# Six weight splits of each mixture stage placed ahead of the sigmoid and the choice of experts

## The chip, the cores and the metric

The kernel runs on one core of one Trainium2 chip. The metric is the device time of one execution in microseconds (us). An execution is cut by the profiler into the work of the engines: TensorE (PE in the rows, PEld its weight loads), VectorE (DVE), ScalarE (ACT), GpSimd (POOL) and SyncE (SP), which issues most transfers.

## What is computed

x is 4 x 1024 tokens of 256 numbers. Each residual step works on a normalised x:

```
x = x + 0.5 * mixture(layernorm(x))
x = x + attention(layernorm(x))
x = x + 0.5 * mixture(layernorm(x))
x = x + 0.5 * linear(layernorm(x))
x = x + attention_of_16_heads(layernorm(x))
x = x + 0.5 * linear(layernorm(x))

mixture(x):
    scores = sigmoid(x @ w_gate.T)                 # 16 experts, 4 groups of 4
    group  = sum of the two best scores in a group; the 2 best groups are allowed
    w, idx = the 4 best of the allowed scores; w = w / (sum(w) + 1e-6)
    routed = sum over idx of w * (silu(x @ w1.T) * (x @ w3.T)) @ w2.T
    return routed + swiglu of two shared experts
```

The change touches the mixture alone, which runs twice.

## The kernel before, in words

The program is six stages, each ended by a barrier of all engines. Products are made in three passes of a high and a low part of each operand: an operand is rounded into its high part by one engine, and the low part is what is left, subtracted by another. For the weights of a mixture stage this is a **split**: ScalarE copies the staged weights into w_hi (line 532), and GpSimd subtracts w_hi from them into w_lo (line 495). There are 27 loads of 256 KB each (`N_LOADS`), which SyncE issues at line 445 into three staging buffers (`STAGES`), so that load m waits for the low part of load m - 3: `sp.wait_ge(*w_lo(i - STAGES + 2))`.

All engines of a mixture stage follow one list, which `moe_order` writes out; each engine walks through it in order and does its own part of every entry. In it:

- For eight chunks of 512 tokens: norm (DVE, line 185), turn (transposes on PE, line 787; high part by ACT, line 540; low part by DVE, line 705), logit (PE, copied out by ACT at line 546) and back (PE, line 803; copied by DVE, line 709), with three loads and three splits after each of the first seven. Here splits 0 to 20 and loads up to 23 are made.
- sigmoid of all logits (ACT, a table load and one instruction, line 550), which waits for the last copy of line 709.
- route 0, 1 and 2: the choice of groups, of experts and their weights (DVE, lines 584 to 642), prefix: counts by triangular products (PE, lines 811 and 815), place: the slot of each token (DVE, lines 646 to 658). Between them stand unit(0), unit(1), unit(2), which are pieces of the shared experts: up (PE, lines 775 to 777; silu by ACT, line 556, behind a table load of its own; the product by DVE, line 734), turn_h (PE line 862, ACT line 561, DVE line 746) and down (PE; added to x by DVE, line 755).
- loads 24 to 26 and splits 21 to 26. These are the entries that the change moves.
- again and scatter (DVE lines 697 and 185; POOL, indirect transfers at line 505), table (DVE lines 663 to 674), the rest of the shared experts, and then the tiles of routed tokens, whose first fetch waits for the last w_lo and for all scatters.

DVE's route steps are chained: each waits for the one before it (`then`). The first is held by the sigmoid, PE's prefix by `chosen`, and PE's up(0) stands behind the prefix in PE's queue. The wide attention and the other stages don't use `moe_order`.

Of the kernel before, what the change touches and what calls it, by code (L numbers as in the profile page):

```python
# [110 lines left out]
def macaron(nc, x_d, wg_d, w13_d, w2_d, aq_d, ak_d, av_d, fw_d, fb_d, lq_d, lk_d, lv_d, lo_d,  # L111
# [18 lines left out]
    with ctx:  # L130
# [78 lines left out]
        STAGES, XSLOT, GSLOT = 3, 4, 8  # L209
        N_LOADS = NX + NX // 2  # L210
# [32 lines left out]
        def moe_order(fresh, sums):  # L243


            def unit(i):
                out = [("up", i)] if i < NUNIT else []
                if 0 <= i - 1 < NUNIT:
                    out.append(("turn_h", i - 1))
                j = (i - NSH) // 2 + 2  # L250
                if i >= NSH and (i - NSH) % 2 == 0 and j < SORTED:
                    out.append(("turn_x", j))
                if 0 <= i - 2 < NUNIT:
                    out.append(("down", i - 2))
                return out

            nxt = STAGES

            def loads(n):
                nonlocal nxt  # L260
                out = []
                for _ in range(min(n, N_LOADS - nxt)):
                    out += [("load", nxt), ("split", nxt - STAGES)]
                    nxt += 1
                return out

            def turns(n):
                return [("turn", KD * n), ("turn", KD * n + 1)]

            zeros = [("zero", n) for n in range(len(ZERO_TILES))] if fresh else []  # L270
            order = [("load_gate", 0)] + ([("load_x", b) for b in range(1, BATCH)] if fresh else [])
            order += [("load", m) for m in range(STAGES)]
            for c in range(NCH + 2):
                for n in ([0, 1] if c == 0 else [c + 1]):
                    if n < NCH:
                        if fresh and n % CB == 0:
                            order += [("stat", n // CB), ("root", n // CB)]
                        if n == 0:
                            order.append(("split_gate", 0))
                        order.append(("norm", n))  # L280
                if c < NCH:
                    order += turns(c)
                if 1 <= c < NCH + 1:
                    order.append(("logit", c - 1))
                if c >= 2:
                    order.append(("back", c - 2))
                order += zeros[:1]
                zeros = zeros[1:]
                if c < NCH - 1:
                    order += loads(3)  # L290
            order += [("sigmoid", 0), ("route", 0), ("prefix", 0)] + unit(0) + [("route", 1)] + unit(1)
            order += [("route", 2)] + unit(2) + [("place", 0)] + loads(30) + [
                ("split", m) for m in range(N_LOADS - STAGES, N_LOADS)]
            for c in range(4):
                order += [("again", c), ("scatter", c)]
            order += unit(3) + [("table", 0)]
            for c in range(NCH - 2):
                order += turns(NCH + c) + unit(2 * c + 4)
                if c < 4:
                    order += [("again", c + 4), ("scatter", c + 4)]  # L300
                order += unit(2 * c + 5) if c < NCH - 3 else []
            order += [("fetch", j) for j in range(XSLOT)] + [("turn_x", 0), ("turn_x", 1)] + unit(NSH - 1)
            for i in range(NSH, NUNIT + 2):
                order += unit(i)
                j = (i - NSH) // 2 + XSLOT
                if (i - NSH) % 2 and j < SORTED:
                    order.append(("fetch", j))
            if sums:
                for t in range(NT):
                    order += [("gather", t), ("combine", t)]  # L310
            return order

        def moe(fresh, routing, sums):
            order = moe_order(fresh, sums)
            gate_ring = Ring([u for u in order if u[0] in ("logit", "back") or u[0] == "turn" and u[1] < KD * NCH],
                             [psum[:, i, :] for i in range(6)])
# [2091 lines left out]
```

How the kernel before makes its waits and increments, by code:

```python
def macaron(nc, x_d, wg_d, w13_d, w2_d, aq_d, ak_d, av_d, fw_d, fb_d, lq_d, lk_d, lv_d, lo_d,  # L111
# [31 lines left out]
        def then(ins):  # L143
            ins.then_inc(*chain.up())
            dve.wait_ge(*chain.now())
# [1 line left out]
        def end_of_stage(n, kept=()):  # L148
            done = S("stage_done")
            act.activation(sd[0:1, 0:1], ident[0:1, 0:1], ACT.Sqrt)
            for e in (pe, act, dve, pool, sp):
                e.drain().then_inc(*done.up())
            for e in (pe, act, dve, pool, sp):
                e.wait_ge(*done.now())
            S.next_stage(kept)
# [13 lines left out]
        def act_root(at, n):  # L170
            act.wait_ge(*S("variance")(n))
            act.activation(sd[:, at], ve[:, at], ACT.Sqrt).then_inc(*S("root").up())
# [1 line left out]
        def dve_rsqrt(at, n, out):  # L174
            dve.wait_ge(*S("root")(n))
            then(dve.reciprocal(recip[:, at], sd[:, at]))
            then(dve.tensor_tensor(newton[:, at], recip[:, at], recip[:, at], ALU.mult))
            then(dve.tensor_tensor(newton[:, at], newton[:, at], ve[:, at], ALU.mult))
            then(dve.tensor_scalar(newton[:, at], newton[:, at], -0.5, 1.5, ALU.mult, ALU.add))
            then(dve.tensor_tensor(out[:, at], recip[:, at], newton[:, at], ALU.mult))
# [13 lines left out]
        pool.memset(ident[:, :], 0.0).then_inc(*S("const").up())
        pool.wait_ge(*S("const")(1))
        pool.affine_select(out=ident[:, :], in_=ident[:, :], compare_op=ALU.not_equal, fill=1.0, base=0,
# [1217 lines left out]
                def on_dve():  # L1415
# [48 lines left out]
                            dve.wait_ge(*ulp_ok(c + first))
```

## Time and profile before

| | us |
|---|---|
| median of 3 runs | 2512.88 |
| lowest and highest | 2509.45, 2513.04 |
| the profiled execution's own time | 2509.05 |
| its span, first to last instruction | 2507.3 |
| busy PE, DVE, ACT, POOL | 2107.8, 1532.2, 954.3, 308.9 |
| mean granted TensorE clock, as a share of full | 0.905 |

The span is shorter than the execution's time by 1.75 us of start and end. Busy times are sums over stages with different limits: the stretch in question is two times some 55 us, in which PE idles much. Times in rows are counted from the span's start; the first mixture stage's choice of experts lies at 61 to 105 us, the second's at 946 to 989 us.

### The profile page before, as it was taken

What the parts mean: (1) busy time and instruction counts of PE and PEld (TensorE: products, weight loads), DVE (VectorE), ACT (ScalarE), POOL (GpSimd) and SP (SyncE); (2) the same over time, 40 slices, a digit from 0 to 9 for tenths busy, and PEclk for the clock granted to TensorE, in tenths of its full rate; (3) what the DMA queues carried; (4) which work ended last, traced back from release to release, by engine and by line L of the source; (5) the groups of instructions that cost most, each with busy time, mean ns of one, the idle gap of its engine ahead of it and who ended that gap; (6) DMA issues with size and microseconds to landing.
All of it is one profiled execution on the core that took longest, in us unless ns stands there. A gap on an engine that the chain in (4) does not pass through costs nothing.

```text
span 2507.3 us, 37607 instructions
## 1 busy us (share of the span) xinstructions
PE 2107.8 (84%) x13066; PEld 1605.4 (64%) x13066; DVE 1532.2 (61%) x3628; ACT 954.3 (38%) x1765; POOL 308.9 (12%) x280
## 2 busy tenths in 40 slices
PE   5589999966999974899999736759999899899757
PEld 3478888855888953788888624625555455555445
DVE  7744334346555577444334399677788687688386
ACT  4122233222333342233223234306656556556532
POOL 4320000022000033300000151211101101100000
PEclk8799999988999996999999856679999999999956
DMA  8120111111000031201111130162242332422001
GB/s 265 41 67 25 30 27 31 29 51 42 1 1 1 1 98 50 78 20 31 29 29 31 44 94 9 38 89 52 53 52 53 62 42 53 70 34 28 4 24 51
DMA packets 84026, 114.77 MB, mean 46 GB/s; under 512 B 12212, under 2 KB 73816, under 8 KB 80728
## 3 DMA queue, kind: packets, MB, share of 16 engines
q1 hardware_dynamic: 77416, 94.80, 17.3%
q0 software_dynamic: 6432, 17.57, 2.2%
q8 instruction: 115, 1.88, 0.3%
q14 instruction: 63, 0.52, 0.1%
HBM read 69.16 MB, written 43.17 MB: 45 GB/s over the span
## 4 chain that ended last, share of the span: by engine, by line
PE 67%; DVE 20%; ACT 5%; DMA 3%; issue 3%; POOL 2%; SPq 0%; ACTq 0%; POOLq 0%; DVEq 0%
PE psum L775 10%; PE psum L777 10%; PE psum L776 10%; PE psum L126 5%; PE psum L2316 5%; PE psum L2295 4%; PE psum L127 4%; PE psum L128 4%; PE psum L2267 4%; PE psum L862 3%; DVE m L2178 2%; DVE stats L160 2%; PE psum L2299 2%; DVE xn L185 2%; PE psum L2271 2%
## 5 line engine op out<-in xcount | busy, mean ns | idle before, releaser
L740 DVE SCALAR_TENSOR_TENSOR h<-psum,xg,sg 128x128 f32<-128x128 f32 x592 | 166.8, 345 | 415.3 <-PE psum L862 415.3
L2142 ACT ACTIVATE pt<-psum 128x512 f32<-128x512 f32 x576 | 315.5, 597 | 241.1 <-DVE psum L2220 147.3
L2178 DVE TENSOR_REDUCE m<-psum 128x1 f32<-128x512 f32 (+2 forms) x576 | 377.8, 683 | 39.8 <-PE psum L2267 33.4
L556 ACT ACTIVATE sg<-psum 128x512 f32<-128x512 f32 x180 | 107.7, 598 | 574.6 <-PE psum L777 574.6
L775 PE MATMUL psum<-w_hi,xt_hi 128*128 (+1 forms) x720 | 285.8, 397 | 32.8 <-DVE xt_lo L705 32.8
L776 PE MATMUL psum<-w_lo,xt_hi 128*128 (+1 forms) x720 | 283.9, 394 | 0.0
L777 PE MATMUL psum<-w_hi,xt_lo 128*128 (+1 forms) x720 | 283.8, 394 | 0.0
L2267 PE MATMUL psum<-ks,qs 96*128 96x512 bf16 (+3 forms) x768 | 242.7, 338 | 24.4 <-DMA ks<-qk_scr 12.4
L2295 PE MATMUL psum<-qs,ks 99*128 99x512 bf16 (+3 forms) x768 | 234.8, 331 | 11.4 <-ACT pt L2142 6.6
L775 PE MATMUL psum<-w_hi,ht_hi 128*128 (+1 forms) x720 | 218.1, 303 | 0.3
L777 PE MATMUL psum<-w_hi,ht_lo 128*128 (+1 forms) x720 | 204.0, 283 | 0.0
L776 PE MATMUL psum<-w_lo,ht_hi 128*128 (+1 forms) x720 | 202.7, 282 | 0.0
L775 PEld LDWEIGHTS psum<-w_hi,xt_hi 128*128 128x128 f32 x720 | 136.9, 190 | 58.9 <-issue 35.7
L2295 PEld LDWEIGHTS psum<-qs,ks 99*128 99x128 bf16 x768 | 69.3, 98 | 154.2 <-ACT pt L2142 95.3
L777 PEld LDWEIGHTS psum<-w_hi,xt_lo 128*128 128x128 f32 x720 | 136.6, 190 | 29.9
L776 PEld LDWEIGHTS psum<-w_lo,xt_hi 128*128 128x128 f32 x720 | 137.1, 190 | 22.8
L2316 PE MATMUL psum<-pt,v 128*17 128x512 f32 (+3 forms) x1536 | 151.5, 490 | 0.0
L776 PEld LDWEIGHTS psum<-w_lo,ht_hi 128*128 128x128 f32 x720 | 137.3, 191 | 0.0
L775 PEld LDWEIGHTS psum<-w_hi,ht_hi 128*128 128x128 f32 x720 | 136.7, 190 | 0.6 <-issue 0.6
L777 PEld LDWEIGHTS psum<-w_hi,ht_lo 128*128 128x128 f32 x720 | 136.5, 190 | 0.0
L2271 PE MATMUL psum<-band_q,ident_q 128*128 128x256 bf16 (+1 forms) x512 | 136.0, 272 | 0.0
L2299 PE MATMUL psum<-band,ident_r 128*128 128x256 f32 (+1 forms) x576 | 135.7, 337 | 0.0
(285 smaller groups left out, 4298.8 us busy)
## 6 DMA issues: line engine op xcount, KB each, us to landing
xg<-w_dram SPq DMA_DIRECT2D x54, 256.0 KB, 3.2
qk_scr<-parts SPq DMA_DIRECT2D x32, 384.0 KB, 2.5
qs<-qk_scr SPq DMA_DIRECT2D x96, 128.0 KB, 7.1
ks<-qk_scr SPq DMA_DIRECT2D x96, 128.0 KB, 7.7
xg<-rows_in SPq DMA_DIRECT2D x74, 132.0 KB, 2.2
rows_out<-yb SPq DMA_DIRECT2D x74, 128.0 KB, 1.7
x<-x_dram SPq DMA_DIRECT2D x4, 1024.0 KB, 8.9
out_dram<-x SPq DMA_DIRECT2D x4, 1024.0 KB, 4.5
```

Source lines behind the costliest of these rows:

```text
L126: pe.matmul(out, ai(ah), bi(bh), start=first, stop=False)
L740: ins = dve.scalar_tensor_tensor(out=h[i % 2][:, e, :], in0=u[:, e, :], scalar=xg[j % XSLOT][:, at:at + 1], in1=sg[i % 2][:, e, :], op0=AL ...
L775: pe.matmul(out, a[0], b[0], start=first, stop=False)
L776: pe.matmul(out, a[0], b[1], start=False, stop=False)
L777: return pe.matmul(out, a[1], b[0], start=False, stop=last)
L2142: act.activation(pt[n % NPT][:, :], st_bank(n), ACT.Exp).then_inc(*exped.up())
L2178: dve.tensor_reduce(m3[:, h, at:at + (n - 1) * step + 1:step], mx_ring.bank((kind, i)).rearrange("p (n k) -> p n k", k=wide), AXIS.X, ALU. ...
L2267: ins = pe.matmul(bank[:, o:o + c1 - c0], qs[r][0:KS_ROWS, h, t * P:(t + 1) * P], ks[r][0:KS_ROWS, h, c0:c1], start=True, stop=not near)
L2271: ins = pe.matmul(bank[:, o + w - bw - c0:o + w - c0], tables.ident_q[:, :], band_q[:, u % NHG * HG + h, 2 * P - bw:2 * P], start=False, s ...
L2295: ins = pe.matmul(bank[:, o:o + wide], ks[r][:, h, j * P:(j + 1) * P], qs[r][:, h, q0:q0 + wide], start=True, stop=not by_pe)
L2299: ins = pe.matmul(bank[:, o:o + near], tables.ident_r[:, :], band[:, part, u % NHG, h, b0:b0 + near], start=False, stop=(part == 1))
L2316: ins = pe.matmul(y_banks[c][h * MQ:h * MQ + DH + 1, BANK - wide:BANK], v1[b % 2][:, j, g * HG + h, :], slot[:, o:o + wide], start=(j == F ...
```

## The change

Loads 24 to 26 and splits 21 to 26 come directly after the eight chunks, ahead of the sigmoid, in both mixture stages (the same code makes both). Nothing is added or taken away.

```diff
                 if c < NCH - 1:
                     order += loads(3)
+            order += loads(30) + [("split", m) for m in range(N_LOADS - STAGES, N_LOADS)]
             order += [("sigmoid", 0), ("route", 0), ("prefix", 0)] + unit(0) + [("route", 1)] + unit(1)
-            order += [("route", 2)] + unit(2) + [("place", 0)] + loads(30) + [
-                ("split", m) for m in range(N_LOADS - STAGES, N_LOADS)]
+            order += [("route", 2)] + unit(2) + [("place", 0)]
             for c in range(4):
```

`loads(30)` gives what is left, three loads with splits 21 to 23; the list behind it adds splits 24 to 26.

The queues of PE, DVE, POOL and SP hold the same instructions in the same order as before, since none of these engines has other work between the two places that the splits or loads would pass. Only ACT's queue differs. The first difference, in the first mixture stage at the end of the chunks (line 550 is the sigmoid, and w_in0 to w_in2 are the semaphores of the three staging buffers' loads):

```order
 L540 ACTIVATE xt_hi<-psum 128x512 [waits turned,logit] x2
 L546 ACTIVATE logit_t<-psum 16x512 [waits logit,backed] x2
+L532 ACTIVATE w_hi<-xg 128x512 [waits w_in0]
+L532 ACTIVATE w_hi<-xg 128x512 [waits w_in1]
+L532 ACTIVATE w_hi<-xg 128x512 [waits w_in2]
+L532 ACTIVATE w_hi<-xg 128x512 [waits w_in0]
+L532 ACTIVATE w_hi<-xg 128x512 [waits w_in1]
+L532 ACTIVATE w_hi<-xg 128x512 [waits w_in2]
 L550 ACT_TABLE_LOAD
 L550 ACTIVATE xn<-logits 128x512 [waits logit_ok]
```

The six copies now stand between the last copy of logits and the sigmoid with its table load. The second difference, in the same stage where they stood (sg is the silu of up(2) and up(3), ht_hi the high part of turn_h(1) and turn_h(2)):

```order
 L556 ACTIVATE sg_30<-psum 128x512 [waits up,su]
 L561 ACTIVATE ht_hi<-psum 128x512 [waits h_turned]
-L532 ACTIVATE w_hi<-xg 128x512 [waits w_in0]
-L532 ACTIVATE w_hi<-xg 128x512 [waits w_in1]
-L532 ACTIVATE w_hi<-xg 128x512 [waits w_in2]
-L532 ACTIVATE w_hi<-xg 128x512 [waits w_in0]
-L532 ACTIVATE w_hi<-xg 128x512 [waits w_in1]
-L532 ACTIVATE w_hi<-xg 128x512 [waits w_in2]
 L556 ACTIVATE sg_31<-psum 128x512 [waits up,su]
 L561 ACTIVATE ht_hi<-psum 128x512 [waits h_turned,down]
```

The silu of up(3) now follows turn_h(1) directly. The second mixture stage shows the same two differences.

## Rows read from the trace of the kernel before

**Rows 1.** Stretches: window, us, busy PE PEld DVE ACT POOL, PEclk, DMA share, GB/s
```profile
100.00:116.00 16.00, 5.65 (x24) 4.95 (x24) 15.45 (x50) 1.79 (x3) 6.91 (x7) 0.50 0.14 51
```

**Rows 2.** Chain of work, first stage's sigmoid: start us, us, what
```profile
61.16 0.59 ACT logit_t L546
...
61.76 1.28 ACT L550
...
63.06 0.64 ACT xn L550
...
63.79 0.42 DVE xn L584
```

**Rows 3.** Timeline of SyncE, loads 21 to 23: start us, us, what
```profile
57.27 2.79 SPq L445 DMA_DIRECT2D xg<-w_dram  x3
```

**Rows 4.** Timeline of ACT, first stage, splits 21 to 26
```profile
86.44 1.66 ACT L532 ACTIVATE w_hi<-xg 128x512 fp32r<-128x512 f32 x3
91.23 0.63 ACT L532 ACTIVATE w_hi<-xg 128x512 fp32r<-128x512 f32 x1 [3.13 <-DMA xg<-w_dram]
...
93.94 0.63 ACT L532 ACTIVATE w_hi<-xg 128x512 fp32r<-128x512 f32 x1 [0.59 <-DMA xg<-w_dram]
94.48 0.58 ACT L556 ACTIVATE sg<-psum 128x512 f32<-128x512 f32 x1
```

**Rows 5.** Timeline of ACT, second stage, the same splits
```profile
970.94 1.66 ACT L532 ACTIVATE w_hi<-xg 128x512 fp32r<-128x512 f32 x3
...
978.58 0.63 ACT L532 ACTIVATE w_hi<-xg 128x512 fp32r<-128x512 f32 x1 [0.80 <-DMA xg<-w_dram]
```

**Rows 6.** Timeline of POOL, first stage, low parts of splits 21 to 26
```profile
87.14 3.77 POOL L495 TENSOR_TENSOR w_lo<-xg,w_hi 128x512 fp32r<-128x512 f32 x3 [27.43 <-ACT w_hi L532]
91.94 1.26 POOL L495 TENSOR_TENSOR w_lo<-xg,w_hi 128x512 fp32r<-128x512 f32 x1 [1.02 <-ACT w_hi L532]
93.44 2.66 POOL L495 TENSOR_TENSOR w_lo<-xg,w_hi 128x512 fp32r<-128x512 f32 x2 [0.23 <-ACT w_hi L532]
```

**Rows 7.** Chain of work, first stage, route 2 on DVE
```profile
89.84 1.12 DVE logit_t L626
...
92.10 1.65 DVE xn L630
...
93.83 1.12 DVE xn L632
...
94.97 1.22 DVE xn L634
...
96.21 0.23 DVE xn L634
...
98.93 0.70 DVE xn L640
```

**Rows 8.** Timeline of DVE, second stage, the same steps
```profile
974.35 1.10 DVE L626 TENSOR_SCALAR logit_t<-logit_t 128x32 f32<-128x32 f32 x1
...
976.60 1.64 DVE L630 TENSOR_TENSOR xn<-xn,logit_t 128x512 f32<-128x512 f32 x1
...
978.31 1.10 DVE L632 COPY xn<-xn 128x32 f32<-128x32 f32 x1
...
979.45 1.46 DVE L634 TENSOR_TENSOR xn<-xn 128x32 f32<-128x32 f32 x2
```

**Rows 9.** Chain of work, first stage: prefix, and where matmuls grow short
```profile
70.58 0.33 PE psum L811
...
75.92 0.43 PE psum L777
...
76.86 0.23 PE psum L777
```

**Rows 10.** Closing linear stage: chain by line, 2375 to 2508 us; busy time
```profile
by line: PE psum L126 16.6%; PE psum L1539 11.9%; PE psum L128 9.8%; PE psum L127 9.7%; DVE amax L1445 7.3%; DVE centred L1468 5.2%; DVE xt_lo L1491 4.2%; issue 3.8%; DVE x L1496 3.6%; ACT centred L1396 3.6%; DVE inv L1453 2.2%; DVE centred
...
2400.00:2425.00 25.00, 17.56 (x63) 13.80 (x61) 21.45 (x30) 9.06 (x17) 0.00 (x0) 0.57 0.00 1
```

## The prediction

> **What bounds the kernel now.** I read the stretches first, to see who fills the time after the chunks. Between 100 and 116 us DVE is busy for 15.45 of 16 us while PE works 5.65 [rows 1]: the choice of experts is a chain of DVE steps, and PE, ACT and POOL wait for it. So what counts here is when that chain starts and how fast it runs.
>
> The chain of work shows where it starts. ACT loads the sigmoid's table at 61.76, the sigmoid runs at 63.06, DVE's first step follows at 63.79 [rows 2]. The table load begins the moment ACT is through with the last logits; nothing lies between it and the sigmoid but its own 1.28 us. Anything that is put ahead of it in ACT's queue moves the whole chain, and with it the prefix on PE at 70.58 [rows 9] and up(0), which stands behind the prefix.
>
> Then the timelines of ACT and POOL, for what is moved. In the old place the six copies begin at 86.44 and the last begins at 93.94 for 0.63 us [rows 4], in the second stage 970.94 and 978.58 [rows 5]. Three copies find their data there (1.66 us together); the other three wait, since a staging buffer is loaded again only after its low part is made: POOL takes 3.77 us for three of them [rows 6] and a load needs some 3 us, so that ACT idles 3.13 us ahead of the fourth [rows 4]. Nobody waits for ACT meanwhile: the silu at 94.48 is of up(3), whose product DVE takes up only after route 2 and place.
>
> Last, DVE's steps beside POOL's three pieces of work, 87.14 to 90.9, 91.94 to 93.2 and 93.44 to 96.1 [rows 6]. A subtraction of 128x32 takes 1.12 us, a product of 128x512 1.65, a copy of 128x32 1.12 and a sum of 128x32 1.22, while the next sum of the same form takes 0.23 and a product of 128x512 at 98.93 0.70 [rows 7]. Each of the long ones ends just as a POOL piece ends. The second stage has the same four [rows 8]. DVE is held up by POOL's subtractions here, on the path.
>
> **The change, part by part.**
>
> *The sigmoid's delay.* The six copies now run at 61.76, where the table load ran. Loads 21 to 23 were issued from 57.27 within 2.79 us [rows 3], so the third was out at about 59.7, and with 3 us from issue to copy it is there at 62.7, when ACT comes to it (61.76 + 2 x 0.55). Splits 21 to 23 find their data, as before. Splits 24 to 26 wait for POOL and the loads as before, because nothing in that trip depends on the place. So ACT is held for as long as before: 93.94 + 0.63 - 86.44 = 8.13 us in the first stage, 978.58 + 0.63 - 970.94 = 8.27 in the second. Before, the table load began with no gap, so the sigmoid is late by all of it: **16.4 us** in both stages. No work covers it: DVE has nothing between its last logits and the sigmoid, PE's next entry is the prefix, and POOL's next after the splits is the scatter, which needs place. Bounds: if each of the three waiting loads came 0.3 us later than in the old place, 17.0 in all would be the upper end (an estimate from the 2.8 to 3.1 us that the trips take in rows 4 and 6); if the trip had no cost at all, six copies of 0.55 would be left, 3.3 a stage, 6.6 in all. I take 16.4, since it is the same sequence of instructions with the same waits.
>
> *The relief of DVE.* POOL's three pieces move with the copies. They begin 0.7 us after the first copy and end 9.66 us after it (96.10 - 86.44), so at 71.4, while the late sigmoid ends at about 71.8; DVE waits for the sigmoid all that time and loses nothing. In the old place it gets back, first stage: 1.12 - 0.23, 1.65 - 0.70, 1.12 - 0.23 and 1.22 - 0.23, which is 3.72 us [rows 7]; second stage: 1.10 - 0.23, 1.64 - 0.70, 1.10 - 0.23 and 1.46 - 0.46 for the two sums together, 3.68 [rows 8]. Together **7.4 us**. For the subtraction and the copy the short price is that of the nearest step of that size, the 0.23 of the sum. Bounds: 0, if POOL was not the cause, and 8.3 if the short steps took nothing but 0.1. I take 7.4.
>
> *What is late next.* Before, DVE ran without a gap from route 2 to the low parts ahead of the shared experts' next unit; it still does, 8.13 - 3.72 = 4.4 us later. Scatters start from the same chain. The experts' fetches and the last w_lo aren't nearer to the path: w_lo is early by more than before.
>
> *SP and POOL.* Loads 24 to 26 are issued some 25 us earlier, past no other transfer. Nothing.
>
> *PE's clock.* PE idles through all of DVE's first steps, 63.79 to 70.58 [rows 2, 9]; then its matmuls come at 0.43 us until about 76.3, at 0.23 from there [rows 9]: PE starts at the lower of its two levels (1.2 and 2.4 GHz) and rises 5.8 us later. The pause grows by 8 us, and the start is at the lower level again. When exactly it rises may differ: a us earlier or later is worth half a us on the path, and there are four such starts (two a stage), so about 2 us either way. I take 0.
>
> The sum: 16.4 - 7.4 = 9.0 us longer. The profiled execution took 2509.05, 3.8 us under the median; against its own time this gives 2518.1. From the median of 2512.88 it is **2521.9 us**, and I forecast that.
>
> A rule that would make it worse. ACT's table load takes 1.28 us and begins at once behind the last copy, 61.16 + 0.59 [rows 2]. The Trainium skill, ScalarE: Activation LUTs, section What ACT_TABLE_LOAD costs, adds some 1.38 us of drain to a switch of tables. The row shows none, and by that rule the sum would be some 2.8 us larger if the drain were hidden before and isn't now.
>
> **The rivals.**
>
> 1. *DVE's stalls have another cause* (the steps are slow by themselves). Then only the 16.4 us count: 2529.3. Against it: the long steps end with POOL's pieces, and the same forms take 0.23 and 0.70 when POOL rests [rows 6, 7]. 4%.
>
> 2. *A pause in ACT ahead of a table load*, which a long queue of copies brings out: 1.4 us a stage, 2524.7. The rows have no gap, there too behind a copy [rows 2]. 4%.
>
> 3. *No change, because the trip gets cheap.* If loads 24 to 26 were in place when ACT comes to them, 6.6 - 7.4 leaves 0.8 us of gain, 2512.1. POOL's 1.26 us and the load's 3 us stand against it, and SyncE can't issue earlier than the low part is made. 3%.
>
> 4. *No change, because of the clock.* If PE came out of all four pauses at the higher level, it would save at most half of 5.8 us each time, 11.6 us: 2510.3. Longer pauses speak against it. 3%.
>
> 5. *Faster, by the clock of the closing linear stage.* There PE has 48.0% of the chain over 133 us, 64 us, and at 2400 to 2425 us the granted clock is 0.57 though PE is busy 17.56 of 25 us [rows 10]. Matmuls at 0.23 in place of 0.43 [rows 9] would take 30 us off: 2491.9. It decides from where a good half of these matmuls ran at the higher level, since the kernel is faster than before once more than 9.0 us come off, and by over 0.2% from 14. What speaks for it is only that the stage begins 9 us later and that clock and work might fall together otherwise; against it, its pauses come from its own waits and move along. 3%.
>
> That the change doesn't do what it says is ruled out by ACT's queue, which shows it.
>
> **How the numbers follow.** A measurement of this kernel can tell about 0.2%, 5.0 us, from no change: below 2507.9 is faster, up to 2517.9 the same. The forecast has 83%. Of that I put 7 into the band of no change: the three runs lie between 2509.45 and 2513.04, and from the lowest, with 2 us of luck in the clock, it ends at 2516.5. So faster 3% (rival 5), the same 3 + 3 + 7 = 13%, slower 76 + 4 + 4 = 84%. The range goes from 2515.5 (lowest run, 9.0 more, the clock's 2 and 1 us of the relief's upper end less) to 2527 (highest run, 9.0, the clock's 2, rival 2's 2.8); rival 1 and the cases of no change lie outside.
>
> **What would show it.** In the profile after: six copies at line 532 from about 61.8 with idle ahead of the fourth of some 3.1 us; the table load at about 69.9; the prefix at 78.7; lines 626, 630, 632 and 634 at 0.2 to 0.7 us each; the end of the first choice of experts 4.4 us later; and the span some 9 us longer, with all that follows the second choice moved alike. I am wrong if the copies take under 5 us, if the four steps stay at 1.1 to 1.7, or if the second attention or a linear stage changes its length by over 3 us.

## The result and the profile after

The changed kernel takes 2515.74 us (median of 12 runs, 2511.93 to 2520.59). The kernel before, run beside it, takes 2507.95 (12 runs, 2499.69 to 2513.04; the three runs of the table above are among the twelve, and among the slower of them). The ratio is 1.0032, with a 95% interval of 1.0021 to 1.0043: 8.0 us slower (5.3 to 10.8). The profiled execution took 2520.59 us with a span of 2518.8, 11.5 more than the span before.

ACT's timeline of the changed kernel, first stage, from the last copy of logits on (start us, us, then the instruction), which answers to [rows 2, 4]:

```profile
63.59 0.59 ACT L546 ACTIVATE logit_t<-psum 16x512 f32<-16x512 f32 x1 [3.34 <-PE psum L777]
64.09 1.65 ACT L532 ACTIVATE w_hi<-xg 128x512 fp32r<-128x512 f32 x3
68.88 0.63 ACT L532 ACTIVATE w_hi<-xg 128x512 fp32r<-128x512 f32 x1 [3.14 <-DMA xg<-w_dram]
...
71.64 0.63 ACT L532 ACTIVATE w_hi<-xg 128x512 fp32r<-128x512 f32 x1 [0.74 <-DMA xg<-w_dram]
72.29 1.28 ACT L550 ACT_TABLE_LOAD   x1
73.58 0.63 ACT L550 ACTIVATE xn<-logits 128x512 f32<-128x512 f32 x1
```

The six copies stand where the table load stood, with the same idle time ahead of the fourth (3.14 us; 3.13 in [rows 4]). From the start of the last logits copy to the table load it was 61.76 - 61.16 = 0.60 us [rows 2]; now it is 72.29 - 63.59 = 8.70. That is 8.10 us of delay. The second stage, in the same view:

```profile
950.42 0.59 ACT L546 ACTIVATE logit_t<-psum 16x512 f32<-16x512 f32 x1 [3.09 <-PE psum L777]
...
959.14 1.28 ACT L550 ACT_TABLE_LOAD   x1
```

Here it is 8.72 us, where the trace before has 0.60: 8.12 of delay. What DVE got back, in the chain of work of the changed kernel, first stage, route 2 (start us, us, what), against [rows 7]:

```profile
99.37 0.19 DVE logit_t L626
...
100.70 0.69 DVE xn L630
...
101.47 0.17 DVE xn L632
...
101.66 0.23 DVE xn L634
...
102.16 0.30 DVE xn L636
```

All four long steps are short. From line 626 to line 636 it takes 102.16 - 99.37 = 2.79 us; before it took 6.62 in the first stage and 6.59 in the second, and the second stage of the changed kernel has 2.79 too. So 3.83 and 3.80 us came back. The chain also shows the prefix and up(0), which answer to [rows 9]:

```profile
81.10 0.32 PE psum L811
...
84.11 0.63 PE psum L775
84.74 0.24 PE psum L776
```

PE still starts at the lower level, but matmuls grow short (0.24 us for 0.43) 3.6 us after the prefix began and not 5.8, which shortens the way from the prefix to the first silu from 7.23 to 6.23 us; in the second stage from 6.82 to 6.47.

From the last logits copy to the first matmul after the choice of experts the first stage takes 58.32 us (55.05 before), the second 58.18 (54.52): 3.27 and 3.66 longer, 6.9 together. Of the profiled pair's 11.5 us, 4.6 are left, and they lie outside the two choices of experts. Most of them are at the end. First the chain of the kernel before, the last products, then that of the changed kernel:

```profile
2497.07 0.35 PE psum L1539
...
2498.32 0.31 PE psum L1539
2498.63 0.32 PE psum L126
```

```profile
2504.17 0.55 PE psum L1539
...
2506.30 0.51 PE psum L1539
2506.80 0.51 PE psum L126
```

The same matmuls go at the higher level in one execution and at the lower in the other. From the first of these last products to DVE's addition behind them it takes 8.42 us (2504.17 to 2512.59) for 4.93 (2497.07 to 2502.00), 3.5 more, and the last transfer out takes 5.42 us for 4.47. The last 12 us of the kernel before are thus 4.4 longer. Another 2.4 us arose ahead of the first sigmoid, in the chunks; 1.4 were won back between the two choices of experts and 0.9 between the second choice and those last 12 us.

The end doesn't follow the change. In the nine traces of this case the time from the first of the last products to the end is 10.2 us (before, e1, e4), 11.7 (e5), 12.2 (e7), 12.7 (e3, e6), 14.7 (the change) and 15.2 (e2): the longest is in a kernel that is as fast as the one before, and one of the shortest in a kernel that is slower than the change. The 2.4 us in the chunks are of the same kind: the first stage's last logits copy begins at 61.2 us before, at 63.6 with the change and at 61.4 to 62.6 in the other seven. Such differences between executions are in the spread of the 12 runs on either side, and so in the interval.

### The profile page after: what moved, and what is told of

Read it like the earlier page. It is cut to its first block, busy times and chain, and to the rows that moved or that the text cites. A ratio compares the mean times of both kernels' runs of the same rounds, so it can differ in the third digit from the quotient of the medians.

```text
span 2518.8 us, 37607 instructions
## 1 busy us (share of the span) xinstructions
PE 2112.3 (84%) x13066; PEld 1607.8 (64%) x13066; DVE 1523.0 (60%) x3628; ACT 954.4 (38%) x1765; POOL 308.5 (12%) x280
## 4 chain that ended last, share of the span: by engine, by line
PE 68%; DVE 19%; ACT 5%; DMA 4%; issue 2%; POOL 2%; SPq 0%; ACTq 0%; DVEq 0%; POOLq 0%
PE psum L775 10%; PE psum L777 10%; PE psum L776 10%; PE psum L126 5%; PE psum L2316 5%; PE psum L2295 4%; PE psum L128 4%; PE psum L127 4%; PE psum L2267 4%; PE psum L862 3%; DVE m L2178 2%; DVE stats L160 2%; PE psum L2299 2%; DVE xn L185 2%; PE psum L2271 2%
## 5 line engine op out<-in xcount | busy, mean ns | idle before, releaser
L2267 PE MATMUL psum<-ks,qs 96*128 96x512 bf16 (+3 forms) x768 | 243.6, 339 | 26.1 <-DMA ks<-qk_scr 12.7
```

What stands on the lines that cost most here:

```text
L2267: ins = pe.matmul(bank[:, o:o + c1 - c0], qs[r][0:KS_ROWS, h, t * P:(t + 1) * P], ks[r][0:KS_ROWS, h, c0:c1], start=True, stop=not near)
```

## The experiments

The experiments were timed beside the kernel before, which took 2505.77 (27 runs) with e1 to e4 and 2505.65 (17 runs) with e5 to e7. The last column is the ratio with its 95% interval, in us of that time. The edits of e1 to e6 are shown against the changed kernel, that of e7 against the kernel before.

| kernel | median us | ratio | us against before |
|---|---|---|---|
| the change | 2515.74 | 1.0032 | +8.0 (5.3 to 10.8) |
| e1: sigmoid ahead of the splits | 2510.14 | 1.0015 | +3.8 (1.3 to 6.3) |
| e2: three splits ahead, three behind | 2505.94 | 0.9997 | -0.8 (-3.5 to 2.3) |
| e3: six splits in the shared experts | 2498.78 | 0.9969 | -7.8 (-10.5 to -4.8) |
| e4: the change, POOL busy beside route 2 | 2521.33 | 1.0059 | +14.8 (10.0 to 19.5) |
| e5: the change in the first stage alone | 2510.03 | 1.0013 | +3.3 (0.5 to 6.0) |
| e6: nine splits in the shared experts | 2497.76 | 0.9961 | -9.8 (-12.8 to -6.8) |
| e7: before, sigmoid held for 8 us | 2521.26 | 1.0055 | +13.8 (10.5 to 17.0) |

**e7, the delay alone.** ACT's part of the sigmoid in the kernel before:

```diff
                         elif kind == "sigmoid":
+                            act.wait_ge(*w_hi(22))
+                            for n in range(12):
+                                act.activation(sg[0][:, :, :].rearrange("p e f -> p (e f)"),
+                                               w13[0][:, 0, 0:512].bitcast(F32), ACT.Copy).then_inc(*S("held").up())
+                                act.wait_ge(*S("held").now())
                             act.wait_ge(*logit_ok(NCH))
```

> The kernel before with twelve chained copies of 128x512 on ACT ahead of the sigmoid in both stages (they write a tile that silu overwrites; nothing else is changed), so that the table load is some 8 us late while loads, splits and POOL's work stay in their old place. By my theory this is the change without its relief: 16 us slower than before, with the four steps at 1.1 to 1.7 us as before. If something takes up part of a late sigmoid (work that gets done meanwhile, PE's clock), it is clearly less than 16.

Measured: 13.8 us slower (10.5 to 17.0). ACT's timeline, first stage:

```profile
61.41 0.59 ACT L546 ACTIVATE logit_t<-psum 16x512 f32<-16x512 f32 x1 [2.18 <-PE psum L782]
61.91 7.89 ACT L551 ACTIVATE sg<-w_hi 128x512 f32<-128x512 f32 x12
69.81 1.28 ACT L555 ACT_TABLE_LOAD   x1
```

and the chain, first stage (lines are 5 higher than in the kernel before; the rows are the steps of lines 626, 630, 632, 634):

```profile
96.95 1.11 DVE logit_t L631
...
99.20 1.63 DVE xn L635
...
100.91 1.11 DVE xn L637
...
102.05 1.22 DVE xn L639
```

The table load is 69.81 - 61.41 - 0.60 = 7.80 us late, in both stages, 15.6 together, and the four steps are as long as before. The interval holds the whole 15.6 and excludes anything under 10.5: most of the delay reaches the end, and nothing is seen that covers a late sigmoid.

**e4, the relief taken back.** In the changed kernel POOL gets eight subtractions, which clear a staging buffer that is read by nobody any more:

```diff
+                        elif kind == "route" and i == 2:
+                            pool.wait_ge(*su(2))
+                            for n in range(8):
+                                pool.tensor_tensor(xg_room[:, 0:2 * D], xg_room[:, 0:2 * D], xg_room[:, 0:2 * D],
+                                                   ALU.subtract).then_inc(*S("spare").up())
+                                pool.wait_ge(*S("spare").now())
```

> The change, with eight subtractions of 128x512 on POOL added beside route 1 and 2 (they clear a staging buffer that is no longer needed; the result is used by nobody). ACT's copies and the transfers stay ahead of the sigmoid. If POOL holds up DVE's four steps of lines 626, 630, 632 and 634, these take 1.1 to 1.7 us again, and the kernel is 3 to 5 us a stage slower than the change, some 14 to 18 slower than before. If the copies on ACT or the loads were the cause, the steps stay at 0.2 to 0.7 us and the time is that of the change, 8 us slower than before. The steps of line 624 should stay at 4.6 us in either case, as they did.

Measured: 14.8 us slower than before, 6.8 more than the change. POOL's timeline and then the chain, first stage (lines 6 higher: the steps of lines 624, 626, 628, 630, 632):

```profile
92.73 9.52 POOL L499 TENSOR_TENSOR xg<-xg 128x512 f32<-128x512 f32 x8 [21.16 <-DVE h L740]
```

```profile
93.24 4.62 DVE xn L630 x32
97.89 0.40 DVE logit_t L632
...
98.70 1.22 DVE xn L634
99.94 1.41 DVE xn L636
...
101.43 0.89 DVE xn L638
```

Only POOL's work was added there, and DVE's steps grew again: line 628 from 0.70 to 1.22, line 630 from 0.69 to 1.41, line 632 from 0.17 to 0.89. The stretch from line 626 to 636 is 4.95 us for 2.79, 2.2 more a stage and not the 3 to 5 expected (POOL's pieces ended at 102.25, and line 626 met the end of one; line 634 was free again). Each of the long steps again ends with a piece or a fixed time behind one: line 630's ends at 101.35, and the piece that it met ran from 99.44 to 100.81. Direction and cause are clear. The size is 4.3 us by the trace (the second stage's steps are as long as the first's), against 6.8 between two measured times that are uncertain by 4.8 and 2.8. The 32 steps of line 624 take 4.62 us with POOL beside them and 4.63 in the changed kernel without: they are not held up.

**e1, the sigmoid first.**

```diff
-            order += loads(30) + [("split", m) for m in range(N_LOADS - STAGES, N_LOADS)]
-            order += [("sigmoid", 0), ("route", 0), ("prefix", 0)] + unit(0) + [("route", 1)] + unit(1)
+            order += [("sigmoid", 0)] + loads(30) + [("split", m) for m in range(N_LOADS - STAGES, N_LOADS)]
+            order += [("route", 0), ("prefix", 0)] + unit(0) + [("route", 1)] + unit(1)
```

> The change, but with the sigmoid's entry ahead of the six splits and three loads; route 0 follows behind them. Only ACT's queue differs from the change. If the change costs time because ACT's queue holds the sigmoid (my theory), the sigmoid's table load is back at some 0.6 us behind the start of the last logits copy (8.7 in the change), and the time falls from the change's by 2 x 8.1 us less what POOL's subtractions, now beside route 0, cost DVE there. If such stalls hit every DVE step with operands in SBUF, route 0 takes 3 to 5 us more a stage: 5 to 9 us better than the change less 0 to 2, that is 0 to 5 us faster than the kernel before. If the steps of route 0 are spared, 7 us faster than before. The rival, that the loads or POOL themselves are what the sigmoid waits for, has no gain over the change.

Measured: 3.8 us slower than before, 4 faster than the change. This missed the expectation of 0 to 5 faster. POOL's timeline and the chain, first stage:

```profile
65.21 3.93 POOL L495 TENSOR_TENSOR w_lo<-xg,w_hi 128x512 fp32r<-128x512 f32 x3 [4.79 <-ACT w_hi L532]
70.12 5.01 POOL L495 TENSOR_TENSOR w_lo<-xg,w_hi 128x512 fp32r<-128x512 f32 x3 [0.98 <-ACT w_hi L532]
```

```profile
64.72 0.43 DVE xn L584
...
65.52 1.24 DVE xn L586
...
66.75 1.28 DVE xn L587
...
70.67 1.69 DVE xn L592
...
72.38 1.65 DVE xn L593
...
77.42 0.32 PE psum L811
```

The sigmoid is in time (the table load is 0.60 us behind the start of the last logits copy). But from DVE's first step to the prefix it takes 12.70 us where it took 70.58 - 63.79 = 6.79 [rows 2, 9]: 5.9 us a stage are lost beside POOL here, against 3.8 in the old place. All of these steps take two operands from SBUF. 2 x (5.9 - 3.8) = 4.2 us is near the measured slowdown of 3.8 (1.3 to 6.3). In the trace the way from the prefix to the first silu is besides 1.3 us shorter in the first stage and 0.3 longer in the second than before, by the clock. POOL is held up too: its last three pieces take 5.01 us, where three without a wait between them take 3.77 in [rows 6]. What failed is the size of the stall, not the delay: without the late sigmoid this version is faster than the change though it stalls more.

**e2, three and three.**

```diff
-            order += loads(30) + [("split", m) for m in range(N_LOADS - STAGES, N_LOADS)]
+            order += loads(30)
             order += [("sigmoid", 0), ("route", 0), ("prefix", 0)] + unit(0) + [("route", 1)] + unit(1)
             order += [("route", 2)] + unit(2) + [("place", 0)]
+            order += [("split", m) for m in range(N_LOADS - STAGES, N_LOADS)]
```

> Only the three splits whose data are in place (21 to 23) and loads 24 to 26 come ahead of the sigmoid; splits 24 to 26 stay in their old place. If the sigmoid's delay is six copies plus the trip of a refill, then with three copies and no trip it is 1.7 us a stage. In the old place three copies find their data and POOL works one piece of 3.8 us there, which by the theory of the shared port delays only the step of line 626 (about 0.9 us): relief 2.9 us a stage. Together 2.4 us faster than before. The rival, that a delay comes from having copies there at all and not from the trip, expects about 4 us a stage of delay and 2 us slower than before.

Measured: 0.8 us faster, with an interval (3.5 faster to 2.3 slower) that holds zero, the 2.4 faster expected and the rival's 2 slower. The time decides nothing here; the trace does. The chain, first stage (lines 1 higher):

```profile
61.65 0.59 ACT logit_t L547
62.23 1.56 ACT w_hi L533 x3
63.81 1.28 ACT L551
...
65.84 0.98 DVE xn L585
...
92.54 1.12 DVE logit_t L627
...
94.79 0.69 DVE xn L631
```

Three copies without a trip delay the table load by 63.81 - 61.65 - 0.60 = 1.56 us, as expected, and not by the rival's 4. In the old place only line 626's step is still long, as expected, so 2.9 of the 3.8 us come back. The term that was missing is at 65.84: POOL is now beside DVE's first step, 0.98 for 0.42. The trace gives 1.56 + 0.56 - 2.9 = -0.8 us a stage, 1.6 us faster in all.

**e5, one stage.** The new place in the first stage (`fresh`), the old one in the second:

```diff
-            order += loads(30) + [("split", m) for m in range(N_LOADS - STAGES, N_LOADS)]
+            moved = fresh
+            if moved:
+                order += loads(30) + [("split", m) for m in range(N_LOADS - STAGES, N_LOADS)]
             order += [("sigmoid", 0), ("route", 0), ("prefix", 0)] + unit(0) + [("route", 1)] + unit(1)
             order += [("route", 2)] + unit(2) + [("place", 0)]
+            if not moved:
+                order += loads(30) + [("split", m) for m in range(N_LOADS - STAGES, N_LOADS)]
```

> The change in the first mixture stage alone; the second keeps the old order. The two stages cost the same by my theory (sigmoid 8.1 us late, 3.8 us of DVE's stalls gone), so this is half of the change: some 4 us slower than before, and in the second stage the four steps of lines 626 to 634 are long again and the table load starts 0.6 us after the start of the last logits copy. The rival, that the first stage alone is to blame (it also clears the rows and loads x, its transfers being 250 GB/s and more), expects all 8 us.

Measured: 3.3 us slower (0.5 to 6.0), which holds 4 and excludes 8. ACT's timeline, table loads of the first and the second stage:

```profile
71.08 1.28 ACT L554 ACT_TABLE_LOAD   x1
...
948.91 1.28 ACT L554 ACT_TABLE_LOAD   x1
```

The first comes 8.7 us behind the start of the last logits copy at 62.38, the second 0.6 behind the one at 948.30. Half of the change's 8.0 us fits, and the rival, that the first stage alone is to blame, doesn't.

**e3, the splits spread late.** No split in the choice of experts; instead, in the rounds of the shared experts:

```diff
-            order += loads(30) + [("split", m) for m in range(N_LOADS - STAGES, N_LOADS)]
...
             for c in range(NCH - 2):
+                order += loads(3) if c == 0 else []
+                order += [("split", N_LOADS - STAGES + c - 2)] if 2 <= c <= STAGES + 1 else []
                 order += turns(NCH + c) + unit(2 * c + 4)
```

> The six splits leave the choice of experts altogether: splits 21 to 23 and loads 24 to 26 stand behind table, splits 24 to 26 one by one in the later rounds of the shared experts, where PE sets the time and ACT and DVE have gaps. By my theory the relief is kept (3.8 us a stage) and the sigmoid isn't late: 7.6 us faster than before, about 15 faster than the change. The rival is that POOL's pieces delay the scatters and with them the first fetch (166.8 us before, needed at some 180) or DVE's steps in the shared experts: then the gain is under 4 us. If the stalls had another cause than POOL, there is no gain.

Measured: 7.8 us faster than before (4.8 to 10.5), as expected. It beats both kernels. POOL's timeline and SyncE's, first stage:

```profile
123.77 3.73 POOL L496 TENSOR_TENSOR w_lo<-xg,w_hi 128x512 fp32r<-128x512 f32 x3
...
161.55 1.28 POOL L496 TENSOR_TENSOR w_lo<-xg,w_hi 128x512 fp32r<-128x512 f32 x1
```

```profile
163.09 31.43 SPq L474 DMA_DIRECT2D xg<-rows_in  x5
```

POOL's pieces stand between scatters; the first fetch goes out at 163.09, where it was 166.79 in the kernel before. DVE's stretch from line 626 to 636 takes 2.79 us (89.97 to 92.76).

**e6, nine splits late.** As e3, with three splits fewer in the chunks; the nine are dealt out over the rounds of the shared experts:

```diff
-                if c < NCH - 1:
+                if c < NCH - 1 and c != 4:
                     order += loads(3)
-            order += loads(30) + [("split", m) for m in range(N_LOADS - STAGES, N_LOADS)]
...
             for c in range(NCH - 2):
+                order += loads([2, 1, 1, 1, 0, 0][c])
+                order += [("split", N_LOADS - STAGES + 1)] if c == 4 else []
                 order += turns(NCH + c) + unit(2 * c + 4)
+                order += loads(1) if c == 2 else []
+                order += [("split", m) for m in {3: [N_LOADS - STAGES], 4: [N_LOADS - STAGES + 2]}.get(c, [])]
```

> As the version with the splits spread late (e3), but nine splits: the three of the fifth chunk go late too. If POOL holds DVE at its norm steps of line 185 in the chunks (four took 2.4 to 4.3 us there, 1.4 without POOL) and DVE sets the pace there, a chunk without splits saves 1 to 2.7 us a stage: 2 to 5 us faster than e3, 10 to 13 faster than before. The rival is that the pace in the chunks is set by the loads or by PE's chain, or that POOL becomes late for the scatters: then the same as e3 or slower.

Measured: 9.8 us faster than before (6.8 to 12.8), at the edge of the expected 10 to 13; against e3 the 2.0 us are inside the intervals. In the trace the second stage's norm steps beside the chunk without splits take 1.37 us for four:

```profile
921.38 1.37 DVE L185 TENSOR_SCALAR xn<-x,mean_var,rstd 128x256 f32<-128x256 f32 x4
924.91 3.31 DVE L185 TENSOR_SCALAR xn<-x,mean_var,rstd 128x256 f32<-128x256 f32 x4
```

From the first norm step of the second stage to its table load it takes 42.99 us, 45.34 in e3 and 44.13 in the kernel before, so executions without this edit differ by 1.2 us there. The first stage shows no gain. How much three splits fewer in the chunks are worth is left open.

## Why the prediction was right, and where it was off

*The sigmoid's delay, 16.4 us.* Right. It is 8.10 + 8.12 = 16.2 in the trace, and e7 shows that a delay of 15.6 by other means costs 13.8 (10.5 to 17.0). The refills took the same trip as in the old place.

*The relief, 7.4 us.* Right: 3.83 + 3.80 = 7.6. One reading was loose: of the four long steps three end within 0.1 us of a POOL piece, but line 630's ends at 92.10 + 1.65 = 93.75 [rows 7], 0.55 us behind the piece that ends at 93.2 [rows 6]. The section on the hardware shows that this is part of the pattern. e4 shows POOL as the cause (its work alone, without copies or loads, makes the steps long again), and e3 that the relief is worth 7.8 us where it isn't paid for by a delay. Rival 1 fell with both.

*The pause ahead of a table load.* None: in the new place the load begins at 72.29 behind a copy that ends at 72.27, and the sigmoid 0.01 us behind the load. By the drain that the Trainium skill gives (ScalarE: Activation LUTs, What ACT_TABLE_LOAD costs) it would be some 1.4 us later; the trace doesn't agree. Rival 2 fell.

*The clock, taken as 0 within 2 us.* It gave back 1.0 and 0.35 us ahead of the first silu, and at the two later starts, behind the choice of experts, 0.35 and -0.2 (from the first matmul to the fourth silu it takes 21.45 and 21.81 us, before 21.80 and 21.63). That is inside the bound. Up to those later starts the sum of all terms on the path is 16.2 - 7.6 - 1.35, less 0.3 for small steps, 6.9 us by the two traces; 8.0 was measured and 9.0 forecast, both within the interval of 5.3 to 10.8.

*Rivals 3 to 5.* The trip wasn't cheap, and PE came out of no pause at the higher level. The closing linear stage did differ by its clock, but to the other side in this pair of executions and by 3.5 us, not 30.

*The absolute time.* Forecast 2521.9, measured 2515.7. The step that was off is the base: I started from the median of three runs, 2512.88, and 12 runs beside the changed kernel have 2507.95. The profiled execution's own time plus 9.0, 2518.1, was the nearer figure. That the measured time lies in the range at all is in part luck: the range begins at 2515.5, 0.2 us below it. The band of no change went by the same base, up to 2517.9, and 2515.7 lies inside that band; slower it is only against the 2507.95 timed beside it, by 8.0 us, more than the 5.0 that I took as the resolution.

*The signs.* Copies from 61.8 and the prefix at 78.7 came at 64.1 and 81.1, all by the same 2.4 us that the chunks were longer in that execution; the interval between them was as forecast. The end of the first choice of experts moved by 3.3 us counted from the last logits copy, and not by 4.4, since the clock gave back 1.0. One sign of being wrong did come: a linear stage changed its length by over 3 us, from the second attention's barrier to the end 131.5 us for 127.8. The sign was badly chosen, since this stretch varies by more than that between executions: it takes 126.6 us in e4 and 132.3 in e2, without regard to what these kernels cost.

## What to carry to other kernels

In a list that all engines follow, a step put ahead of another is put there in every queue, and what it waits for (here the refill of a staging buffer) stands in front of whatever that engine does next. Before moving work away from a collision, look at what is the first thing in the new place that has no slack; best is a stretch that another engine bounds, where the moved pieces can be taken one at a time. An engine's steps that grow to another engine's rhythm, and end with its pieces or a fixed time behind them, are a price that can be read from the two timelines side by side.

## What was unexpected in the hardware's behaviour

The loss beside POOL depends on what DVE's steps are: the same six subtractions cost DVE 3.8 us beside route 2 and 5.9 beside route 0, and in the second case POOL lost time as well, 5.01 for 3.77 us. The single pieces show the turns. POOL's last three pieces in e1, first stage, each taken singly from its timeline, go with the steps of lines 592 and 593 shown at e1:

```profile
70.12 1.67 POOL L495 TENSOR_TENSOR w_lo<-xg,w_hi 128x512 fp32r<-128x512 f32 x1 [0.98 <-ACT w_hi L532]
...
71.75 1.71 POOL L495 TENSOR_TENSOR w_lo<-xg,w_hi 128x512 fp32r<-128x512 f32 x1
...
73.43 1.71 POOL L495 TENSOR_TENSOR w_lo<-xg,w_hi 128x512 fp32r<-128x512 f32 x1
```

Line 592's step starts at 70.67, while the piece of 70.12 to 71.79 is under way, and ends 0.55 us behind that piece. POOL's next piece starts at 71.75, while line 592's step is unfinished, and ends 1.1 us behind that step. So it goes on with line 593 (72.38, ends 0.55 behind the piece of 71.75): each engine waits for what the other has under way, and a round takes 1.67 us, in which DVE has 0.70 us of work and POOL 1.26. The same distances are in the other traces: a held step ends 0.04 to 0.07 us behind its piece if it has 128x32 elements, 0.15 if 128x128, 0.28 if 128x256, 0.55 if 128x512 (before, e1, e2, e4, e7). Beside route 0 all six pieces met such a step. Beside route 2 the first two of them ran beside the steps of line 624, which took 4.6 us there and alone, and only four steps were held up.

In the chain of e1 six of the steps of route 0 with two operands in SBUF are 1.2 to 1.7 us long, for 0.2 to 0.7. The Trainium skill, SBUF — State Buffer, section Who interferes with whom, says that a DVE instruction with two inputs in SBUF contends with a GpSimd instruction that reads SBUF, and that the port pair they share is an exclusive lock; the six steps agree with it. Two operands are not the whole of it: the steps of lines 626 and 632 read one tensor each and were held up too, 1.12 us for 0.19 and 0.17.

The spread of the runs, 13 us for the kernel before, is larger than the change. It goes with the granted clock: of the 27 runs beside e1 to e4 the slowest, 2512.91, had a mean of 0.897, and the fastest, 2501.23, one of 0.910. In the pair of traces above, 3.5 us is the clock of the last products.
